# Norms: the reciprocal root by one power on GpSimd in place of logarithm, exponential and a Newton step

## The reference

```python
def _layernorm(x):                                  # layers 0 and 2
    mu = jnp.mean(x, axis=-1, keepdims=True)
    var = jnp.mean(jnp.square(x - mu), axis=-1, keepdims=True)
    return (x - mu) * jax.lax.rsqrt(var + EPS)
def rmsnorm(x, w, eps=EPS):                         # layer 1
    v = jnp.mean(xf * xf, axis=-1, keepdims=True)
    return w * (xf * jax.lax.rsqrt(v + eps))
# layer 0 (layers 1 and 2 alike, with other attentions; layer 1 with silu(h w1) * (h w3))
x = x + g_msa * _attention(_modulate(_layernorm(x), sh_msa, sc_msa), W_qkv, W_out, b_out)
x = x + g_mlp * _ff(_modulate(_layernorm(x), sh_mlp, sc_mlp), W1, b1, W2, b2)
# end of layer 2
x = x + gelu(v_) * tanh(g_) @ tg_out_w.T + tg_out_b
# layer 3: two low-rank products per sequence around a gelu, plus x
```

## Time and profile before

| | |
|---|---|
| time of the runs, median of 3 | 2401.87 us (2399.81 to 2401.93) |
| time of the profiled execution | 2403.36 us |
| its span, first to last instruction | 2401.6 us |
| PE, DVE, ACT, POOL busy | 83%, 66%, 38%, 37% |

### The profile page before, as it was taken

The page is one execution under the profiler, slowest core; times in us unless marked ns, Lnnn a source line. Parts: engine busy times, 40 slices in busy tenths (PEclk is TensorE's granted clock), DMA queues, the critical chain, the costliest instruction groups (busy, mean ns, idle before and its releaser), DMA issues. The chain is left out here.

```text
span 2401.6 us, 41490 instructions
## 1 busy us (share of the span) xinstructions
PE 2005.0 (83%) x15246; PEld 1565.6 (65%) x15246; DVE 1577.4 (66%) x2248; ACT 902.6 (38%) x1480; POOL 877.3 (37%) x787
## 2 busy tenths in 40 slices
PE   4829999999999788867777689896878787888998
PEld 4628878878887566655556567774656566666775
DVE  1136555666656677778888857776778776776554
ACT  0024334444344344434444433332324344443332
POOL 0041110111102444456665823345566564443000
PEclk9959999999999899989898899998989989999999
DMA  7120000000001000010000000001000000000101
GB/s 308 45 70 2 2 2 1 1 2 1 1 2 36 23 0 0 1 40 2 0 0 0 1 24 0 0 1 36 2 0 0 0 1 27 0 0 1 36 0 71
DMA packets 19520, 44.29 MB, mean 18 GB/s; under 512 B 3200, under 2 KB 11200, under 8 KB 18176
## 3 DMA queue, kind: packets, MB, share of 16 engines
q1 hardware_dynamic: 19392, 42.48, 5.1%
HBM read 36.18 MB, written 6.29 MB: 18 GB/s over the span
## 5 line engine op out<-in xcount | busy, mean ns | idle before, releaser
L633 PE MATMUL O<-Ghb,W2b 128*128 128x512 f32 x352 | 148.0, 420 | 83.8 <-DVE Glb L1211 76.2
L523 POOL TENSOR_TENSOR Tm<-Dv,MOD 128x512 f32<-128x512 f32 x96 | 107.4, 1140 | 293.3 <-DVE Dv L580 201.1
L633 PE MATMUL bank<-HH,W1b 128*128 128x512 f32 x448 | 182.3, 407 | 13.2 <-PEq L1479 6.8
L1209 DVE CAST Ghb<-Gfb 128x512 fp32r<-128x512 f32 x176 | 140.3, 797 | 75.0 <-ACT Gfb L1167 49.8
L634 PE MATMUL bank<-HL,W1b 128*128 128x512 f32 x448 | 179.7, 401 | 0.0
L635 PE MATMUL bank<-HH,W1b 128*128 128x512 f32 x448 | 178.9, 399 | 0.0
L1211 DVE TENSOR_TENSOR Glb<-Gfb,Ghb 128x512 fp32r<-128x512 f32 x176 | 174.1, 989 | 6.0
L653 POOL TENSOR_TENSOR spare<-RT 128x1 f32<-128x1 f32 x48 | 9.2, 192 | 440.9 <-DVE RT L644 440.9
L1364 PE MATMUL bank<-WQKa,HH 128*128 128x512 f32 x256 | 101.4, 483 | 80.0 <-DVE HL L588 65.5
L512 POOL TENSOR_TENSOR XS<-Tm 128x512 f32<-128x512 f32 x48 | 64.9, 1353 | 242.1 <-ACT Tm L478 242.1
L633 PEld LDWEIGHTS O<-Ghb,W2b 128*128 128x128 f32 x352 | 66.9, 190 | 126.3 <-DVE Glb L1211 95.5
(11 more groups left out here) (241 smaller groups left out, 5485.2 us busy)
## 6 DMA issues: line engine op xcount, KB each, us to landing
w<-l_w_dram SPq DMA_DIRECT2D x4, 2048.0 KB, 26.3
wm<-w_mods_dram SPq DMA_DIRECT2D x6, 768.0 KB, 11.7
X<-xT_dram SPq DMA_DIRECT2D x4, 1024.0 KB, 36.3
out_dram<-XO SPq DMA_DIRECT2D x8, 512.0 KB, 2.7
W2b_f<-l_w_dram SPq DMA_DIRECT2D x11, 256.0 KB, 5.1
WQK_f<-l_wqk_dram SPq DMA_DIRECT2D x8, 256.0 KB, 6.4
W1b_0f<-l_w_dram SPq DMA_DIRECT2D x8, 256.0 KB, 3.8
b2r<-l_b2r_dram SPq DMA_DIRECT2D x1, 1024.0 KB, 7.2
```

The source lines that it names most:

```text
L523: nc.gpsimd.tensor_tensor(Tm[:, k].rearrange("p (b t) -> p b t", t=T), Dv[:, k].rearrange("p (b t) -> p b t", t=T), m, ALU.mult).then_inc( ...
L633: nc.tensor.matmul(out, w_lo_ap, x_hi, start=first, stop=False)
L1209: nc.vector.tensor_copy(Gh[m % 2][:], gf).then_inc(g_hi.h, 1)
```

## The change

The reciprocal root is computed by one elementwise power on POOL, V3 = V1 ^ V2, with V2 filled once with -0.5. It stands at the head of `pool_h`, ahead of the wait for the product that uses it. Logarithm, exponential, table preload and the Newton step go; `dve_norm` is left with the product.

```diff
--- before.py
+++ after.py
@@ -450,7 +450,7 @@
                             skip = 2 if lead_whole else 0
                             claim(NCH - skip, skip, f_xs, f_xh, f_xl)
                     claim(2 * NCH, 0, f_m)
-                    claim(NCH, 0, f_dd, f_ss, f_sqh, f_sql, f_var, f_v, f_ln, f_rs, f_n1, f_n2, f_n3, f_n, f_h)
+                    claim(NCH, 0, f_dd, f_ss, f_sqh, f_sql, f_var, f_v, f_rs, f_n, f_h)
                 claim(NCH, 0, f_hh, f_hl)
 
             def at(self, c, n):
@@ -483,13 +483,7 @@
                 nc.scalar.activation(FA[:], XS[:], ACT.Copy).then_inc(f_sqh.h, 1)
 
             def act_rstd(self, act, c):
-                if self.preload:
-                    nc.scalar.preload_act_table_set(LN_EXP)
-                act.wait_ge(f_v.h, self.at(f_v, c + 1))
-                act.wait_ge(f_n3.h, self.at(f_n3, c))
-                nc.scalar.activation(V2[:], V1[:], ACT.Ln).then_inc(f_ln.h, 1)
-                act.wait_ge(f_ln.h, self.at(f_ln, c + 1))
-                nc.scalar.activation(V2[:], V2[:], ACT.Exp, scale=-0.5).then_inc(f_rs.h, 1)
+                pass
 
             def act_hh(self, act, c, p):
                 act.wait_ge(f_h.h, self.at(f_h, c + 1))
@@ -517,6 +511,8 @@
 
             def pool_h(self, pool, c, p):
 
+                pool.wait_ge(f_v.h, self.at(f_v, c + 1))
+                nc.gpsimd.tensor_tensor(V3[:], V1[:], V2[:], ALU.pow).then_inc(f_rs.h, 1)
                 pool.wait_ge(f_n.h, self.at(f_n, c + 1))
                 for k in range(DH):
                     m = MOD[self.l][:, self.i_sc, k, bass.ds(c * CB, CB)].unsqueeze(2).to_broadcast([P, CB, T])
@@ -569,12 +565,6 @@
             def dve_norm(self, dve, c):
 
                 dve.wait_ge(f_rs.h, self.at(f_rs, c + 1))
-                nc.vector.scalar_tensor_tensor(out=V3[:], in0=V2[:], scalar=-0.5, in1=V2[:], op0=ALU.mult, op1=ALU.mult).then_inc(f_n1.h, 1)
-                dve.wait_ge(f_n1.h, self.at(f_n1, c + 1))
-                nc.vector.tensor_tensor(V3[:], V3[:], V1[:], ALU.mult).then_inc(f_n2.h, 1)
-                dve.wait_ge(f_n2.h, self.at(f_n2, c + 1))
-                nc.vector.scalar_tensor_tensor(out=V3[:], in0=V3[:], scalar=1.5, in1=V2[:], op0=ALU.add, op1=ALU.mult).then_inc(f_n3.h, 1)
-                dve.wait_ge(f_n3.h, self.at(f_n3, c + 1))
                 r = V3[:].unsqueeze(1).to_broadcast([P, DH, CH])
                 if self.centred:
                     nc.vector.tensor_tensor(Dv[:], Dv[:], r, ALU.mult).then_inc(f_n.h, 1)
@@ -1011,6 +1001,8 @@
 
                     @block.gpsimd
                     def _(pool):
+                        nc.gpsimd.memset(V2[:], -0.5).then_inc(step_a.h, 1)
+                        pool.wait_ge(step_a.h, step_a.at(1))
                         for i in range(2):
                             nc.gpsimd.memset(KB[i][:], 0.0).then_inc(step_p.h, 1)
                             nc.gpsimd.memset(VB[i][:], 0.0).then_inc(step_p.h, 1)
@@ -1037,7 +1029,7 @@
                                 wt.low(pool, wt.all())
                             residual_pool(pool, c)
                         chunks(pool, body)
-                d_in.passed(16); step_p.passed(4)
+                d_in.passed(16); step_p.passed(4); step_a.passed(1)
                 n = NCH * PAIRS
                 for c in (q_ps, k_ps, q_sb, ka_sb, kd_sb, s_ready, s_max, s_sub, p_exp, p_sum, p_rec, pt_ps, pt_sb, o_ps, o_sb,
                           ot_ps, ot_hi, ot_lo, out_ready, v_ps, va_sb, vd_sb):
```

## The result

The changed kernel takes 6168.27 us (median of 4 runs, 6167.87 to 6169.99) beside 2400.84 (2396.65 to 2401.93): 2.5702 times as long, 95% interval 2.5657 to 2.5746. The direction, slower, had the larger chance; the time is almost twice the end of the range, 3160.

A forecast was written before the change was run, and what follows sets the result against it. No engine is full, so queues and waits decide. Powers of 7.9 us less hidden time sum to 197 us, plus about 0.5 for the fill, onto 2403.4; less 1.5 for the median: 2599 us, range 2320 to 3160.

The forecast's parts named there:

- the price of the power: Duration of each of 48 GpSimd powers of 128x512, taken as 7.9 us, with 1.14 and 20.5 for the range.
- 18 steps: Estimated software steps of one power (logarithm, product, exponential): 20.5 us at a whole pass each, 7.9 us in registers.
- 2381 us: Total time if three steps fit one element movement, a power taking 2.75 us; within the faster rival, chance 0.26.
- The rest of the sum: Power's duration less the time hidden at each norm, added over the norms: 197 us more, plus about 0.5 for the fill.
- the four "free" norms: Mainly first norms of the feed-forwards, counted as no loss; GpSimd stands idle 11.61 us before the modulation in such a place.
- 3154 us at p = 20.5: Rival: each step costs a pass or the routine is longer, 751 us more; chance 0.22 for 12 us and more.
- The break-even: Duration of one power at which the change neither gains nor loses by the sum: 3.3 us.
- The covers: Time from a power's possible start to the product's present start, less 0.1 us handoff: 0.5 to 6.8 us by stage.
- an early root would win nothing in attention 0: In attention 0 TensorE is busy 704.09 of 780 us, so an earlier root gains nothing, but a late one costs.
- VectorE held by the power: VectorE's splits at the free norms of b0, b1, b2 are held while the power runs: up to 24 us more, 2623.
- Absorbed waits, rival: Slack in attention chunks and feed-forward splits catching up absorb half of the 197 us: 2500 us, chance 0.1.
- The granted clock: TensorE's clock might fall from 0.95 of the first stage because it stands more; left out of the sum.

The follow-up runs named there:

- plain pass: Changed kernel with its power replaced by a plain GpSimd multiplication of the same size in the same place, root left out: 2328.50 us, ratio 0.9696.
- 48 columns: Changed kernel with its power computed on 48 of the 512 columns, constant 0.25 in the others: 2609.16 us, ratio 1.0863.
- packed: Changed kernel with the 512 values packed into 128x16 by a VectorE block transpose before the power and spread back by another: 2418.09 us, ratio 1.0061.
- packed, early: Power on 128x16 between two VectorE transposes, moved ahead of the previous chunk's residual in attention 0 and feed-forwards: 2340.40 us, ratio 0.9743.
- full, early: Changed kernel with its 128x512 power moved ahead of the residual in GpSimd's queue in attention 0 and feed-forwards: 6063.80 us, ratio 2.5275.

## Why the prediction was wrong

**The step that failed is the price of the power**, as the prediction put it: "I take p = 7.9 us, nearest to the row of the fill, and keep 1.14 and 20.5 for the range." It is 82.2 us. The upper end was no bound: it took 18 steps from a count of mine, "since nothing here shows the routine", and gave each a whole pass; a power costs as much as 72 passes of 1.14, and no run shows what its steps are. Of the trace of before no row could have bounded it from above, so the range had to stay open there, with a larger share of the chance beyond 3160. The estimate worked out from the Trainium skill (GPSIMD Engine Reference, Elementwise — side-by-side cycle accounting: roughly three operations per cycle in longer bodies), 2381 us, fell with it: the row says 82.2 us where that made 2.75.

**The rest of the sum held in total.** With the measured prices in place of p it gives, beside what the runs gave against the kernel before that was run with them:

| p, us | sum, us | measured, us |
|---|---|---|
| 1.10 | -82 | -74 |
| 2.97 | -12 | -24 |
| 8.09 | +206 | +206 |
| 82.2 | +3749 | +3767 |

The last row counts the four "free" norms as well, 82.2 - 11.6 each, since no such place hides 82 us: 1036 + 629 + 926 + 327 + 548 + 282 and 0.5 for the fill. The prediction's 3154 us at p = 20.5 lacks them, 4 x 8.9 = 36 us. The break-even that was put at 3.3 us lies between 2.97 and 8.09; on the straight line between the two it is 3.5.

**The covers, stage by stage.** The distance from one product `Dv` to the next, in the mean over the steps inside each stage (seven in attention 0, six in the feed-forwards, five in attention 1 and 2), worked out from the first and the last start on the timelines:

| kernel | att. 0 | b0 | att. 1 | b1 | att. 2 | b2 |
|---|---|---|---|---|---|---|
| before | 75.87 | 29.17 | 44.36 | 28.16 | 42.06 | 29.19 |
| plain pass | 76.02 | 27.90 | 42.80 | 26.21 | 37.62 | 27.90 |
| 48 columns | 81.12 | 35.37 | 45.05 | 34.45 | 44.37 | 35.35 |
| after | 155.86 | 109.46 | 120.13 | 108.89 | 119.42 | 109.10 |
| packed | 76.48 | 31.13 | 41.61 | 29.06 | 40.76 | 31.03 |
| packed, early | 75.91 | 27.24 | 41.64 | 26.34 | 40.83 | 27.92 |
| full, early | 150.63 | 106.87 | 120.16 | 104.35 | 119.28 | 106.83 |

The growth from before to after is 82.2 less the cover: that leaves 1.9 and 2.3 us in b0 and b2 (said: 2.5), 1.5 in b1 (3.6), 6.4 and 4.8 in attention 1 and 2 (5.0), and 2.2 in attention 0, where five of 2.7 and two of 6.8 (3.9 in the mean) were said. The misses cancel in part. At 48 columns they cancel more: b1 loses 6.3 us a chunk where 4.3 was its term at 7.9, and attention 1 0.7 where 2.9 was. That the total came out to within 1% of the time at 8.09 and 82.2 us is therefore in part luck, and at 2.97 the sum gives only half of the gain. What makes b1's cover 2 us smaller was not tried. That an early root would win nothing in attention 0 was right: 76.0 us a chunk with a plain pass, 75.9 with the packed power ahead of the residual.

**VectorE held by the power: wrong but for its first moments.** The prediction set up to 24 us aside for it, in one thing beside the sum. VectorE's rows inside the power at 1483.18 and at 874.62 have their usual 0.43 and 0.69 us. But a subtraction `Glb` that starts up to 0.4 us behind the start of a power of 128x512 takes 1.66 us: seven times in b1 of the kernel after and 13 times in b0 and b2 with the full power ahead of the residual (1549.88 above). In the same place of b1 beside a power of 48 columns it takes 0.69. So about 1 us is lost at the start of a wide power, not its duration. The rule of the Trainium skill (GPSIMD Engine Reference, Specifications) agrees with that start and with the plain two-input passes L519 (kernel after) and L652 (packed, early), beside which VectorE's operations take two to three times as long (four times beside L655 in the earlier trace rows); it doesn't carry over to the rest of a power.

**Absorbed waits, rival:** at 8.09 us nothing of the sum vanished in total. By the table it holds for attention 1 alone, where the first 8 us of a power cost 0.7 a chunk.

**The granted clock** fell, as the last sentence of the prediction feared: 0.668 of full speed in the mean of the span, from 0.941; both are means between its two levels, 1.2 and 2.4 GHz, and in the kernel after TensorE stands for most of each chunk (74.64 us at one place of the timeline above). Windows over six chunks of b0 show what that is worth (from and to, length, busy us of PE, PEld, DVE, ACT and POOL, granted clock, DMA share, GB/s), first of the kernel before:

```profile
799.00:974.00 175.00, 147.44 (x602) 114.25 (x601) 135.47 (x150) 76.59 (x100) 79.69 (x59) 0.97 0.00 0
```

and of the kernel after:

```profile
1566.00:2222.00 656.00, 154.04 (x600) 120.14 (x600) 122.02 (x132) 54.29 (x76) 572.80 (x65) 0.62 0.00 0
```

TensorE is busy 154.04 us at a granted clock of 0.62 for work that took 147.44 at 0.97, (154.04 - 147.44) / 6 = 1.1 us more a chunk, of which the part behind the product is on the path. That would be enough for the covers' 0.2 to 0.6 us in b0 and b2, but how much of the 18 us that the sum lacks is the clock's was not tried; no kernel of this study holds the clock.

## What to carry to other kernels

Moving an operation to an engine with time to spare is first a question of what that engine takes for this operation; where no row of the trace has it, no range is safe above, and one instruction measured by itself (here 13, in one run) is worth more than any count of steps. The break-even can be forecast without the price: the 3.3 us from the covers, put down before the price was known, lie near the 3.5 of the runs. If the price goes by columns and not by partitions, look for copies of the same value across partitions: packing 512 columns into 16 and starting the power as soon as its input is there turned 2.57 times slower into 2.6% faster.

## What the runs showed of the hardware

A power on GpSimd costs 0.160 us per column of float32 and 0.3 to 0.4 us besides, 82.2 us for 128x512, on 1 partition as on 128, for exponents -0.5, 0.37, 1.0 and 2.0 alike. VectorE's cast and subtraction keep their 0.43 and 0.69 us while it runs, except that a subtraction which starts within 0.4 us of the start of a 128x512 power takes 1.66. A 32x32 block transpose of 128x512 on VectorE takes 0.71 us, from PSUM as from SBUF with a source repeated 32 times along its columns.
